# One core, four sequences: context times Wo added to x as a step of its own, z computed from that sum, and the first attention chain in two halves

## Chip, cores, metric

One core of one Trainium2 chip. The metric is the device time of one launch in microseconds. All data is fp32.

## The reference

Four sequences (B = 4) of 512 tokens with 256 features. Cut to what matters:

```python
# 1. conditioned adapter: h = x + relu(x @ w_down[b]) @ w_up[b], both weights scaled and shifted from cond[b]
# 2. attention on h: paths = sigmoid(h @ Wp + bp); similarity from 5 levels, causal softmax, 8 heads
x = x + (softmax(sim) @ (h @ Wv)) @ Wo
# 3. y = x @ (U[b] @ V) + bias, with U[b] = cond[b] @ W_dec + b_dec, K = 30 inner columns
# 4. each token goes to the expert e with the largest score of y
x = x + y + y @ expert_w[e].T
```

The kernel folds 3 and 4 into a narrow vector z = x @ U + ub of 30 (padded to 32) columns: scores come from z, and the outcome for expert e is z @ G[e], with G[e] = V + V @ expert_w[e].T.

## The kernel before, in words

Everything is kept transposed: features on partitions, tokens on the free axis. `x_t` holds x and, at the end, the output. One list, `ORDER`, fixes the order of all steps, and each of the engines runs through that same list and does its part of each step. So the order of the steps in `ORDER` (built by `after_scores`, `after_context` and a few fixed lists, L76 to L147) is the order of work on each engine.

Attention of a batch is cut into six pairs of key tiles (`PAIRS`, L35), so pair p runs from 0 to 23 and batch b begins at pair 6b. For each: `scores` (TensorE into `s_ps`), Exp (ScalarE into `prob`, L365), where needed a causal mask (GpSimd, L342) or the sum `tiles` (VectorE, "add", L509), and `context` (TensorE into `c_ps`). Four of the six contexts of a batch end a chunk; VectorE then normalises it (reciprocal L420, product L421 into `ctx_t`). Between scores(p+1) and context(p), and behind context(p), stand the other steps, listed in the gaps:

- `gdn`, `gup`: the scaled adapter weights `w_dn`, `w_up` (VectorE adds and multiplies, L432 to L450). `down`, `up`: the adapter, `h_t` on VectorE (L455). `up` comes as two steps, one for each half of the rows of 64.
- `VL`: values and logits of 128 tokens, copied by ScalarE (L377). `bias`, `tanh`, `feat`: logits to 32 products for each head and token (VectorE L464, ScalarE L383, VectorE L549 and L552). `phi`: their transposes for four heads, scaled by ScalarE into `phi_t` (L390). `scores` reads `phi_t`.
- `U`, `Uadd`, `ubT`, `Q`, `G`, `WoU`: once, the weights of the second part. `U` needs W_dec and goes through DRAM. `WoU` is Wo times U.
- `zT`: z of the batch from `x_t` with U and from `ctx_t` with `WoU` (L712), so it needs no sum x + ctx Wo. `zs`: z by token and scores, then on VectorE the copy `z_nat` and the choice (`smax`, `hit`, `key`, `kmax`, `pick`, L519 to L526). `zo`: z placed at the chosen expert (GpSimd, in the last batch VectorE). `zoT`: its transposes, copied by ScalarE to `zo_t` (L402).
- `out` 0 to 3: for one of two feature halves and one of two token halves, `ctx_t` times Wo and `zo_t` times G accumulated in one bank; VectorE adds it to `x_t` in place (L541), and SP stores it.

A step that isn't scores or context writes a PSUM bank. Behind the start only two banks are left for them, taken in turn (`WORK`, L149 to L158). TensorE waits before a step until the last user of its bank has been emptied (`emptied`), that is read by VectorE or ScalarE. In the start four banks of `s_ps` serve as well (`EARLY_BANK`); scores(0) waits until they are emptied.

## Time and profile before

| | us |
|---|---|
| median of 3 runs | 154.97 (154.96 to 156.26) |
| the profiled execution | 155.55 |
| its span | 153.4 |

| engine | busy us | share |
|---|---|---|
| TensorE | 141.2 | 92% |
| VectorE | 83.7 | 55% |
| ScalarE | 58.8 | 38% |
| GpSimd | 31.2 | 20% |

The profiled execution is one run; its span is the time from the first to the last event on the core, and 2.15 us lie around it. PE is TensorE, PEld its weight loads, DVE VectorE, ACT ScalarE, POOL GpSimd, SP the engine that issues loads and stores. Matmuls all go through helper functions, so they carry line L561 and are told apart by their tiles: `work<-w_vl,h_t` is VL, `work<-ctx_t,mix_sb` the first half of `out`, `work<-zo_t,gexp` its second half. Each fp32 matmul shows as two rows, except transposes. Their ends are modelled and run on into the next step, so the length of a step is best read from start to start. "idle before <- X" says what ended the engine's wait.

### The profile page before, as it was taken

How to read it: one execution, taken by the hardware profiler on the slowest of the kernel's cores; microseconds unless marked ns; L12 is line 12 of the kernel's file. 1: busy time of each engine (PE TensorE's matmuls, PEld its weight loads, DVE VectorE, ACT ScalarE, POOL GpSimd, SP SyncE). 2: the span in 40 equal slices, each digit the busy share in tenths (PEclk: the TensorE clock that was granted, in tenths of full speed). 3: DMA queues.
4: the chain of work that ended last, by engine and by line, in shares of the span. 5: the costliest groups of instructions: out<-in, count | busy, mean ns of one | idle time of the engine just before them, and what ended most of it. 6: DMA issues, size and time to landing. Idle time of an engine off the chain costs nothing.

```text
span 153.4 us, 5078 instructions
## 1 busy us (share of the span) xinstructions
PE 141.2 (92%) x2296; PEld 89.8 (59%) x2296; DVE 83.7 (55%) x156; ACT 58.8 (38%) x70; POOL 31.2 (20%) x56
## 2 busy tenths in 40 slices
PE   5989678999497999999999999999999999999992
PEld 5746155554274777457656655567558577666650
DVE  0563532619966378296915483558146851985431
ACT  3013156264226342558333451573434447310010
POOL 7200004100405302640022205200222440110000
...
GB/s 121 311 320 433 448 376 353 209 4 0 0 22 17 35 0 4 0 4 0 37 3 38 34 4 0 38 0 4 34 38 38 0 38 0 38 38 34 68 38 71
DMA packets 7381, 12.50 MB, mean 81 GB/s; under 512 B 1552, under 2 KB 5808, under 8 KB 7232
## 3 DMA queue, kind: packets, MB, share of 16 engines
...
q0 software_dynamic: 96, 0.05, 1.1%
...
q14 instruction: 3, 0.02, 0.1%
...
## 4 chain that ended last, share of the span: by engine, by line
PE 83%; DVE 11%; ACT 2%; issue 1%; POOL 0%; ACTq 0%; POOLq 0%; DVEq 0%
PE work L561 36%; PE c_ps L561 24%; PE s_ps L561 17%; PE work L738 3%; DVE rden L420 2%; DVE feat L552 2%; PE work L678 2%; DVE tiles L509 1%; ACT prob L365 1%; DVE h_t L455 1%; ACT phi_t L390 1%; DVE u_row L481 1%; PE work L730 1%; DVE x_t L541 1%; DVE logit L464 0%
## 5 line engine op out<-in xcount | busy, mean ns | idle before, releaser
L365 ACT ACTIVATE prob<-s_ps 128x1536 f32<-128x1536 f32 (+1 forms) x24 | 38.2, 1593 | 39.3 <-PE s_ps L561 36.3
L420 DVE RECIPROCAL rden<-c_ps 128x256 f32<-128x256 f32 x16 | 28.1, 1757 | 26.5 <-PE c_ps L561 26.5
L342 POOL TENSOR_SCALAR_AFFINE_SELECT prob<-prob 128x1024 f32<-128x1024 f32 x16 | 20.1, 1257 | 93.1 <-ACT prob L365 93.1
L561 PE MATMUL s_ps<-phi_t 32*128 32x256 f32 (+1 forms) x384 | 24.2, 365 | 1.6 <-ACT phi_t L390 1.0
L561 PE MATMUL c_ps<-prob,v_sb 128*32 128x256 f32 (+1 forms) x384 | 24.9, 346 | 0.0
L561 PEld LDWEIGHTS s_ps<-phi_t 32*128 32x128 f32 x384 | 17.4, 184 | 10.6 <-issue 6.8
L561 PE MATMUL work<-ctx_t,mix_sb 128*32 128x256 f32 x256 | 17.0, 381 | 0.4
L561 PE MATMUL work<-zo_t,gexp 128*32 128x256 f32 x256 | 16.9, 379 | 0.0
L561 PEld LDWEIGHTS c_ps<-prob,v_sb 128*32 128x32 f32 x384 | 11.5, 109 | 9.0 <-issue 2.0
L561 PE MATMUL c_ps<-prob,ones 128*32 128x256 f32 (+1 forms) x256 | 16.3, 326 | 0.0
L561 PE MATMUL work<-w_vl,h_t 128*32 128x296 f32 x208 | 14.8, 416 | 1.1 <-DVE h_t L455 0.6
L541 DVE TENSOR_TENSOR x_t<-work,x_t 128x256 f32<-128x256 f32 x16 | 6.7, 419 | 13.3 <-PE work L561 13.3
L561 PEld LDWEIGHTS work<-zo_t,gexp 128*32 128x32 f32 x256 | 8.6, 110 | 5.2 <-ACT zo_t L402 0.2
L561 PEld LDWEIGHTS work<-ctx_t,mix_sb 128*32 128x32 f32 x256 | 7.8, 110 | 4.9 <-ACT phi_t L390 1.2
L509 DVE TENSOR_TENSOR tiles<-prob 128x1024 f32<-128x1024 f32 x8 | 10.6, 1329 | 0.0
L561 PEld LDWEIGHTS work<-w_vl,h_t 128*32 128x32 f32 x208 | 6.1, 109 | 7.1 <-DVE pick L526 1.6
L561 PEld LDWEIGHTS c_ps<-prob,ones 128*32 128x32 f32 x256 | 8.0, 110 | 2.7
L350 POOL TENSOR_TENSOR zo<-z_nat,pick 128x256 f32<-128x256 f32 x12 | 7.0, 615 | 9.8 <-DVE pick L526 9.8
L377 ACT COPY v_sb<-work 128x296 f32<-128x296 f32 x13 | 5.2, 403 | 9.6 <-PE work L561 9.6
L455 DVE TENSOR_TENSOR h_t<-work,x_t 128x512 f32<-128x512 f32 x6 | 3.9, 686 | 8.2 <-PE work L561 8.2
L402 ACT COPY zo_t<-work 128x512 f32<-128x512 f32 x8 | 4.4, 590 | 8.4 <-PE work L738 8.4
L421 DVE TENSOR_TENSOR ctx_t<-c_ps,rden 128x256 f32<-128x256 f32 x16 | 6.8, 424 | 0.6
...
## 6 DMA issues: line engine op xcount, KB each, us to landing
...
```

The lines of the kernel that those rows point to most:

```text
L342: nc.gpsimd.affine_select(out=tri, in_=tri, compare_op=ALU.is_ge, fill=0.0, base=0, pattern=[[0, HG], [0, 2], [1, P]], channel_multiplier= ...
L350: ins = nc.gpsimd.tensor_tensor(zo[:, t], z_nat[:, t:t + 1, :].broadcast_to([P, E, KP]), pick[:, t, :].unsqueeze(2).broadcast_to([P, E, KP ...
L365: nc.scalar.activation(prob[:, p % 2, :, 0:width(p)], s_ps[:, :, 0:width(p)], ACT.Exp).then_inc(exped, 1)
L377: nc.scalar.copy(v_sb[:, b % 2, t, :], bank(s)[:, 0:D + H * DEPTH]).then_inc(empty(s), 1)
L402: nc.scalar.copy(zo_t[:, :, CW * s[2]:CW * (s[2] + 1)], bank(s)[:].rearrange("p (e t) -> p e t", e=2)).then_inc(empty(s), 1)
L420: link(nc.vector.reciprocal(rden[:], c_ps[m % 2][:, CW:2 * CW]))
L421: nc.vector.tensor_tensor(ctx_t[:, b % 2, g, CW * half:CW * (half + 1)], c_ps[m % 2][:, 0:CW], rden[:], ALU.mult).then_inc(ctx_ready, 1)
L455: nc.vector.tensor_tensor(h_t[:, :, half], bank(s)[:].rearrange("p (c t) -> p c t", c=DC), x_t[:, b, :, half], ALU.add).then_inc(empty(s), 1)
L509: nc.vector.tensor_tensor(tiles[:, chunk(p) % 2], both[:, :, 0, :], both[:, :, 1, :], ALU.add).then_inc(added, 1)
L541: nc.vector.tensor_tensor(x_t[:, b, c, half], bank(s)[:, 0:CW], x_t[:, b, c, half], ALU.add).then_inc(empty(s), 1)
L561: return nc.tensor.matmul(o, w, r, start=start, stop=stop, skip_group_check=True)
L738: ins = nc.tensor.transpose(o[:, CW * e + P * i:CW * e + P * (i + 1)], zo[:, 2 * hf + i, 4 * e:4 * e + 4, :].rearrange("p e k -> p (e k)") ...
```

## The change

- `WoU`, its transposed copy of Wo and the `ctx_t` half of `zT` are gone. `out` is cut in two steps. `mix` multiplies `ctx_t` by Wo and adds the result to `x_t` in place; `zT` reads `x_t` once all `mix` steps of its tokens have been added; `out` holds only `zo_t` times G, and adds again. Each `mix` and `out` takes a bank and a VectorE add.
- The first batch's `bias`, `tanh`, `feat` and `phi` come in two halves, for the first and the last 256 tokens. The first pair of scores needs only the first. The second half's `phi` stand behind scores 1, in front of `up` of batch 1.
- Scaling of `phi` goes to VectorE for group 1 in all batches, and for both groups of the first batch's second half.
- `gdn` of batches 1 to 3 runs as two VectorE instructions of 384 columns in place of six of 128, and stands before `up`; `gup` 1 stands behind it. `gup` 2 and 3 move out of the start into batch 0. `U`, `G` and VL of batch 1 change their gaps.
- W_dec, mix and the expert weights are loaded on SP's queue behind x of batch 1, and no longer by ScalarE behind its first `down`; x of batches 2 and 3 follow them. mix is 256 KB smaller.
- Eight warm-up products in place of nine, and the two banks are taken in the other turn.

```diff
-WARM = 9
+WARM = 8
...
-PROLOGUE = [("gdn", (0,)), ("gup", 0), ("down", 0), ("gup", 1), ("up", 0, 0), ("up", 0, 1), ("gdn", (1, 2, 3)),
-            ("VL", 0, 0), ("VL", 0, 1), ("VL", 0, 2), ("VL", 0, 3), ("bias", 0), ("tanh", 0), ("feat", 0),
-            ("gup", 2), ("gup", 3), ("phi", 0, 0), ("phi", 0, 1), ("scores", 0), ("down", 1)]
-EARLY_BANK = {("gdn", (0,)): 0, ("gup", 0): 1, ("down", 0): 2, ("gup", 1): 3, ("up", 0, 0): 4, ("up", 0, 1): 5,
-              ("gdn", (1, 2, 3)): 0, ("VL", 0, 0): 1, ("VL", 0, 1): 2, ("VL", 0, 2): 3, ("VL", 0, 3): 4,
-              ("gup", 2): 0, ("gup", 3): 1, ("phi", 0, 0): 5, ("phi", 0, 1): 2}
+def part(b, ts):
+
+    return 1 if ts == FIRST else b + 2
+
+
+def scaler(s):
+
+    return "scalar" if s[2] == 0 and s[3] != SECOND else "vector"
+
+
+def features(b, ts):
+
+    return [("bias", b, ts), ("tanh", b, ts), ("feat", b, ts)]
+
+
+PROLOGUE = [("gdn", (0,)), ("gup", 0), ("down", 0), ("gdn", (1, 2, 3)), ("up", 0, 0), ("up", 0, 1), ("gup", 1),
+            ("VL", 0, 0), ("VL", 0, 1), *features(0, FIRST), ("VL", 0, 2), ("VL", 0, 3), ("bias", 0, SECOND),
+            ("phi", 0, 0, FIRST), ("phi", 0, 1, FIRST), ("tanh", 0, SECOND), ("scores", 0), ("feat", 0, SECOND),
+            ("down", 1)]
+EARLY_BANK = {("gdn", (0,)): 0, ("gup", 0): 1, ("down", 0): 2, ("gdn", (1, 2, 3)): 3, ("up", 0, 0): 4, ("up", 0, 1): 5,
+              ("gup", 1): 0, ("VL", 0, 0): 1, ("VL", 0, 1): 2, ("VL", 0, 2): 4, ("VL", 0, 3): 5,
+              ("phi", 0, 0, FIRST): 1, ("phi", 0, 1, FIRST): 2}
 def after_scores(b):
...
-        gaps[4] += [("phi", n1, 0), ("phi", n1, 1)]
+        gaps[4] += [("phi", n1, 0, ALL_T), ("phi", n1, 1, ALL_T)]
     if b == 0:
-        gaps[1] += [("VL", n1, 2), ("VL", n1, 3)]
-        gaps[2] += [("U", 1)]
+        gaps[0] = [("phi", b, 0, SECOND), ("phi", b, 1, SECOND)] + gaps[0]
+        gaps[1] += [("U", 1)]
+        gaps[2] += [("VL", n1, 2), ("VL", n1, 3)]
         gaps[3] += [("U", 3)]
-        gaps[5] += [("G", 1), ("Uadd",)]
+        gaps[5] += [("gup", 3), ("Uadd",)]
     elif n1 < B:
         gaps[1] += [("zs", prv, ALL_T), ("zo", prv, 0), ("zo", prv, 1), ("VL", n1, 0), ("VL", n1, 1)]
         gaps[2] += [("VL", n1, 2), ("VL", n1, 3)]
@@ -101,6 +118,7 @@
         gaps[1] += [("zs", prv, ALL_T), ("zo", prv, 0), ("zo", prv, 1)]
         gaps[4] += [("zs", b, FIRST), ("zo", b, 0)]
     if prv >= 0:
+        gaps[0] += [("mix", prv, 2), ("mix", prv, 3)]
...
 def after_context(b):
...
-        gaps[0] += [("VL", n1, 0), ("VL", n1, 1)]
-        gaps[1] += [("bias", n1), ("tanh", n1), ("U", 0), ("feat", n1)]
-        gaps[2] += [("U", 2)]
-        gaps[3] += [("Q",)]
-        gaps[4] += [("G", 0), ("ubT",)]
-        gaps[5] += [("down", n2), ("WoU",)]
+        gaps[0] += [("U", 0)]
+        gaps[1] += [("VL", n1, 0), ("VL", n1, 1)]
+        gaps[2] += features(n1, ALL_T) + [("U", 2)]
+        gaps[3] += [("Q",), ("gup", n2)]
+        gaps[4] += [("G", 0), ("ubT",), ("mix", b, 0)]
+        gaps[5] += [("G", 1), ("down", n2), ("mix", b, 1)]
     else:
         gaps[0] += [("zT", prv, ALL_T)]
-        gaps[3] += [("out", prv, 0)]
-        gaps[4] += [("out", prv, 1)]
-        gaps[5] += [("out", prv, 2)]
+        gaps[2] += [("mix", b, 0), ("mix", b, 1)]
     if b >= 1 and n1 < B:
-        gaps[2] += [("bias", n1), ("tanh", n1), ("feat", n1)]
-    if prv >= 1:
-        gaps[1] += [("out", prv - 1, 3)]
+        gaps[2] += features(n1, ALL_T)
+        gaps[3] += [("out", prv, 0), ("out", prv, 1)]
+        gaps[4] += [("out", prv, 2)]
+        gaps[5] += [("out", prv, 3)]
     if b >= 1 and n2 < B:
         gaps[5] += [("down", n2)]
     if b == B - 1:
-        gaps[2] += [("zT", b, FIRST)]
-        gaps[5] = [("zoT", b, 0), ("out", prv, 2), ("out", prv, 3)]
+        gaps[3] += [("zT", b, FIRST), ("out", prv, 0)]
+        gaps[4] += [("out", prv, 1)]
+        gaps[5] += [("zoT", b, 0), ("out", prv, 2), ("out", prv, 3)]
...
-ORDER += [("zT", B - 1, SECOND), ("out", B - 1, 0), ("zs", B - 1, SECOND), ("zo", B - 1, 1),
-          ("out", B - 1, 1), ("zoT", B - 1, 1), ("out", B - 1, 2), ("out", B - 1, 3)]
+ORDER += [("out", B - 1, 0), ("mix", B - 1, 2), ("mix", B - 1, 3), ("out", B - 1, 1), ("zT", B - 1, SECOND),
+          ("zs", B - 1, SECOND), ("zo", B - 1, 1), ("zoT", B - 1, 1), ("out", B - 1, 2), ("out", B - 1, 3)]
...
-        _k, _late = _late % 2, _late + 1
+        _k, _late = 1 - _late % 2, _late + 1
...
-            for b in range(1, B):
+            sp.dma_start(x_t[:, 1], x_tr[1].rearrange("(c p) t -> p c t", p=P)).then_inc(ld_x[1], 16)
+            sp.dma_start(wdec[:], W_dec).then_inc(ld_wdec, 16)
+            sp.dma_start(mix_sb[:], mix).then_inc(ld_mix, 16)
+            sp.dma_start(ex_t[:], expert_tr.rearrange("e (c p) f -> p e c f", p=P)).then_inc(ld_ex, 16)
+            for b in range(2, B):
                 sp.dma_start(x_t[:, b], x_tr[b].rearrange("(c p) t -> p c t", p=P)).then_inc(ld_x[b], 16)
...
-                    if s[1] == 0:
-                        act.dma_start(wdec[:], W_dec).then_inc(ld_wdec, 16)
-                        act.dma_start(mix_sb[:], mix).then_inc(ld_mix, 16)
-                        act.dma_start(ex_t[:], expert_tr.rearrange("e (c p) f -> p e c f", p=P)).then_inc(ld_ex, 16)
...
-                elif s[0] == "phi":
-                    _, b, g = s
-                    if b == 0 and g == 0:
+                elif s[0] == "phi" and scaler(s) == "scalar":
+                    _, b, g, ts = s
+                    tok = slice(P * ts[0], P * (ts[-1] + 1))
+                    if b == 0:
                         act.wait_ge(rootc_ready, 1)
                     full(act, s)
-                    nc.scalar.activation(phi_t[:, b % 2, g, :], bank(s)[:], ACT.Copy, scale=rootc[:]
+                    nc.scalar.activation(phi_t[:, b % 2, g, tok], bank(s)[:, tok], ACT.Copy, scale=rootc[:]
...
-                    for b in s[1]:
-                        ins = nc.vector.tensor_tensor(w_dn[:, b], dproj[:],
-                                                      g[:, b:b + 1, 0:HD].broadcast_to([P, DC, HD]), ALU.mult)
-                    link(ins)
-                    for b in s[1]:
-                        ins = nc.vector.tensor_tensor(w_dn[:, b], w_dn[:, b],
-                                                      g[:, b:b + 1, HD:2 * HD].broadcast_to([P, DC, HD]), ALU.add)
-                    ins.then_inc(empty(s), 1)
+                    bs, n = slice(s[1][0], s[1][-1] + 1), len(s[1])
+                    link(nc.vector.tensor_tensor(w_dn[:, bs], dproj[:].unsqueeze(1).broadcast_to([P, n, DC, HD]),
+                                                 g[:, bs, 0:HD].unsqueeze(2).broadcast_to([P, n, DC, HD]), ALU.mult))
+                    nc.vector.tensor_tensor(w_dn[:, bs], w_dn[:, bs],
+                                            g[:, bs, HD:2 * HD].unsqueeze(2).broadcast_to([P, n, DC, HD]), ALU.add
+                                            ).then_inc(empty(s), 1)
...
+                elif kind == "phi" and scaler(s) == "vector":
+                    _, b, g, ts = s
+                    tok = slice(P * ts[0], P * (ts[-1] + 1))
+                    full(dve, s)
+                    nc.vector.tensor_scalar(phi_t[:, b % 2, g, tok], bank(s)[:, tok], rootc[:], None, op0=ALU.mult
+                                            ).then_inc(empty(s), 1)
...
-                elif kind == "WoU":
-                    full(dve, s)
...
-                elif kind == "out":
+                elif kind in ("mix", "out"):
...
-                        done(pe, ("WoU",))
-                    pe.wait_ge(ctx_ready, BC * b + (NG if ts == FIRST else BC))
-                    for c in range(2 * DC):
+                        pe.wait_ge(u_ready, 1)
+                    for i in range(TT):
+                        if i // DC in (t // 2 for t in ts):
+                            done(pe, ("mix", b, i))
+                    for c in range(DC):
                         for t in ts:
-                            tok = slice(P * t, P * (t + 1))
-                            w = u_w[:, c, b, :] if c < DC else wo_u[:, c - DC, KP * b:KP * (b + 1)]
-                            r = x_t[:, b, c, tok] if c < DC else ctx_t[:, b % 2, c - DC, tok]
-                            ins = mm(o[KP * t:KP * (t + 1), 0:P], w, r, start=(c == 0), stop=(c == 2 * DC - 1))
+                            ins = mm(o[KP * t:KP * (t + 1), 0:P], u_w[:, c, b, :], x_t[:, b, c, P * t:P * (t + 1)],
+                                     start=(c == 0), stop=(c == DC - 1))
...
-                elif kind == "out":
+                elif kind in ("mix", "out"):
                     _, b, i = s
-                    if b == 0 and i == 0:
-                        done(pe, ("G", 0))
-                        done(pe, ("G", 1))
                     row, half = slice(P * (i % DC), P * (i % DC + 1)), slice(CW * (i // DC), CW * (i // DC + 1))
-                    for c in range(2 * DC):
-                        if c == DC:
-                            done(pe, ("zoT", b, i // DC))
-                        w = wo[:, c, row] if c < DC else gexp[:, c - DC, row]
-                        r = ctx_t[:, b % 2, c, half] if c < DC else zo_t[:, c - DC, half]
-                        ins = tiled(o[:, 0:CW], w, r, start=(c == 0), stop=(c == 2 * DC - 1))
+                    if kind == "mix":
+                        if b == 0 and i == 0:
+                            pe.wait_ge(ld_mix, 16)
+                        pe.wait_ge(ctx_ready, BC * b + NG * (i // DC + 1))
+                    else:
+                        if b == 0 and i == 0:
+                            done(pe, ("G", 0))
+                            done(pe, ("G", 1))
+                        done(pe, ("zoT", b, i // DC))
+                    for c in range(DC):
+                        w = wo[:, c, row] if kind == "mix" else gexp[:, c, row]
+                        r = ctx_t[:, b % 2, c, half] if kind == "mix" else zo_t[:, c, half]
+                        ins = tiled(o[:, 0:CW], w, r, start=(c == 0), stop=(c == DC - 1))
```

## Rows read from the trace of the kernel before

**Rows 1.** The page: busy us, share of the span, instructions, of TensorE.

```profile
PE 141.2 (92%) x2296; PEld 89.8 (59%) x2296; DVE 83.7 (55%) x156; ACT 58.8 (38%) x70; POOL 31.2 (20%) x56
```

**Rows 2.** Waits, whole span: row waited for; us in total, times, longest.

```profile
PE work L561 <- DVE u_row L481: 2.2, 1, 2.2
...
PE work L678 <- DVE q_bd L470: 1.0, 1, 1.0
...
PE work L561 <- DVE pick L526: 0.5, 2, 0.2
```

**Rows 3.** Timeline of the start: start, duration, engine, tiles, count, idle before and releaser.

```profile
11.66 1.21 PE L561 MATMUL work<-w_vl,h_t 128*32 128x296 f32 x16 [0.59 <-DVE h_t L455]
...
15.78 1.98 PE L561 MATMUL work<-lift_sb,cond_b 128*128 128x512 f32 x4
...
15.91 0.41 ACT L377 COPY v_sb<-s_ps 128x296 f32<-128x296 f32 x1 [0.59 <-PE s_ps L561]
...
19.26 1.06 PE L678 MATMUL s_ps<-ident,feat 128*128 128x128 f32 x8 [1.50 <-DVE feat L552]
...
21.31 0.94 PE L561 MATMUL s_ps<-phi_t 32*128 32x256 f32 x16 [0.98 <-ACT phi_t L390]
...
25.75 0.64 PE L561 MATMUL c_ps<-prob,v_sb 128*32 128x256 f32 x8
```

**Rows 4.** Groups by shape, VectorE: busy us, mean ns; idle before.

```profile
L541 DVE TENSOR_TENSOR x_t<-work,x_t 128x256 f32<-128x256 f32 x16 | 6.7, 419 | 13.3 <-PE work L561 13.3
```

**Rows 5.** Timeline from the end of batch 0 into batch 1.

```profile
54.20 1.06 PE L561 MATMUL work<-u_w,mix_sb 128*32 128x128 f32 x32
...
55.18 0.94 PE L561 MATMUL s_ps<-phi_t 32*128 32x256 f32 x16
...
56.05 1.26 PE L561 MATMUL work<-act_t,w_up 64*128 64x256 f32 x8
...
57.21 1.29 DVE L455 TENSOR_TENSOR h_t<-work,x_t 128x512 f32<-128x512 f32 x2 [1.08 <-PE work L561]
...
57.24 0.64 PE L561 MATMUL c_ps<-prob,v_sb 128*32 128x256 f32 x8
...
58.82 1.76 DVE L420 RECIPROCAL rden<-c_ps 128x256 f32<-128x256 f32 x1 [0.32 <-PE c_ps L561]
...
59.00 0.62 PE L561 MATMUL work<-ctx_t,wo_u 128*32 128x128 f32 x16
...
62.48 1.20 PE L561 MATMUL work<-w_vl,h_t 128*32 128x296 f32 x16 [0.24 <-DVE pick L526]
```

**Rows 6.** The page: GB/s of all transfers in 40 slices of 3.8 us.

```profile
GB/s 121 311 320 433 448 376 353 209 4 0 0 22 17 35 0 4 0 4 0 37 3 38 34 4 0 38 0 4 34 38 38 0 38 0 38 38 34 68 38 71
```

**Rows 7.** Timeline: the two halves of one `out` step.

```profile
72.62 1.05 PE L561 MATMUL work<-ctx_t,mix_sb 128*32 128x256 f32 x16
...
73.49 1.05 PE L561 MATMUL work<-zo_t,gexp 128*32 128x256 f32 x16
```

**Rows 8.** Timeline of the last batch, where GpSimd and VectorE meet.

```profile
133.79 1.10 POOL L342 TENSOR_SCALAR_AFFINE_SELECT prob<-prob 128x1024 f32<-128x1024 f32 x1 [7.31 <-ACT prob L365]
...
133.81 1.10 DVE L524 TENSOR_TENSOR key<-hit,rank 128x16 f32<-128x16 f32 x1
```

**Rows 9.** Timeline of the tail.

```profile
136.98 0.66 PE L738 MATMUL work<-ident,zo 128*128 128x128 f32 x4
...
144.25 0.23 DVE L519 COPY z_nat<-work 128x64 f32<-128x64 f32 x1
...
145.42 0.76 DVE L534 TENSOR_TENSOR zo<-z_nat,pick 128x256 f32<-128x256 f32 x2
...
146.99 0.59 ACT L402 COPY zo_t<-work 128x512 f32<-128x512 f32 x1 [4.48 <-PE work L738]
...
150.61 0.42 DVE L541 TENSOR_TENSOR x_t<-work,x_t 128x256 f32<-128x256 f32 x1 [1.30 <-PE work L561]
```

**Rows 10.** Stretch: length, busy us (count) by engine, granted clock, DMA share, GB/s.

```profile
150.60:153.40 2.80, 0.00 (x0) 0.00 (x0) 0.42 (x1) 0.00 (x0) 0.00 (x0) 0.90 0.15 50
```

67 lines of the change are left out of this document (31 added, 36 removed).

## Prediction, made before the changed kernel was seen

> **What bounds the kernel now.** I read the page first: TensorE is busy for 92% of the span [rows 1], and no other engine comes near. So two things count: how much TensorE has to do, and where it stands still. The list of its waits names the places: 2.2 us for VectorE's copies of `u_row` and 1.0 for `q_bd`, both in batch 0, and 0.5 in two waits of 0.24 for `pick`, one each at the start of batches 2 and 3's VL steps [rows 2]. The timeline of the start shows one more: before the first scores at 21.31 TensorE waits for one long chain, and two `gup` products at 15.78 fill part of that wait for nothing [rows 3]. Behind batch 0 the matmuls follow each other closely, so the rest of the span is almost pure TensorE time.
>
> **Start: the chain is halved.** Four VL steps run from 11.66 to the last copy at 15.91, so one is about 1.0 us, with 0.25 for the pipeline; copy, bias, tanh and the `feat` operations then take until the transposes at 19.26, 3.35 us [rows 3]. Now two VL steps are enough: the copy starts at 11.66 + 2.25 = 13.9. The chain behind it works on half the columns; a little under half of it grows with columns, so I take 2.65 us. In front of it I count 0.3 sooner: one warm-up product less, and `gup` 1 (1.0, half of the 1.98 at 15.78) no longer ahead of `up`, against `w_dn` of three batches that now is, on VectorE. Transposes start at 16.25. From there to the scores took 21.31 - 19.26 = 2.05; half the columns, and a scaling on each of two engines, make it 1.25. First scores: **17.5, 3.8 sooner**. VectorE's scaling of 256 columns isn't in the trace: it lies between 0.42, the in-place add of 256 columns [rows 4], and 0.65, half of the 1.29 of two `h_t` of 512 columns [rows 5]; it is nearest to the first, and I take 0.42.
>
> From the first scores to the first context product took 25.75 - 21.31 = 4.4. The exponential between them stays as it is; the transposes of the second half (0.5), their scaling (0.4, which `up` waits for, as it needs the bank) and the stagger of the second `up` behind the second scaling (0.45) come in: 5.8. First context product at 23.35, **gain 2.4**. Loads: W_dec now stands in SP's queue behind `x` of batch 1. Up to its end 5.8 MB have to move, which at the rates of the slices shown takes until about 19 us [rows 6]; it is wanted first at 24.9. Cost nothing, with 5 us to spare; each us later than 24.9 would count in full.
>
> **TensorE's work.** `WoU` goes: 55.18 - 54.20, with a little before it, 0.9. `zT` loses its `ctx_t` half, 0.62 less the 0.19 by which a row runs on into the next step (1.05 against 73.49 - 72.62): 0.43 in each of five steps, 2.1 [rows 5, 7]. Together 3.0 less. `out` is cut into `mix` and `out`, 0.87 each [rows 7]: no more work, but 16 more adds of 0.42 on VectorE, 6.7 us [rows 4]. `gup` 2 and 3 leave the idle stretch of the start for the full stream: 1.9 more. So TensorE gains only 1 us behind the start. What decides is the waits: every step needs one of two banks, and a bank comes free when VectorE, strictly in order, has emptied it.
>
> **Batch 0, first context product to scores 7** (before 55.18 - 25.75 = 29.4). Work: two `gup` +1.8, `mix` 0 and 1 +1.7, `WoU` -0.9: +2.6. Waits that go: `u_row` 2.2 with 0.3 beside it, `q_bd` 1.0 [rows 2], 0.3 of small ones: -3.8. New ones: a normalisation (reciprocal 1.76, product 0.42) begins 1.6 after its context product does, 58.82 - 57.24 [rows 5]. `phi` 0 of batch 1 needs the bank of `Q`, emptied behind the normalisation and the `q_bd` copies: 0.75; `phi` 1 that of `gup` 2: 0.4. `mix` 0 needs the bank of `G` 0, an add of 0.42 and its latency: 0.6. `mix` 1 needs the bank of `G` 1, whose add stands behind the normalisation of context 5: 0.2 + 2.2 + 0.45 after that context ends, while TensorE has 1.75 to do: 1.1. Sum 2.85. In all 1.65; VectorE operations with two SBUF inputs that meet a mask may add up to 0.9 each [rows 8]. I take **+2.0**.
>
> **Batch boundary, twice** (scores 7 and 13). `up` starts at 56.05, `h_t` at 57.21, 0.65 for each half; before, context follows at 57.24 without any of it [rows 5]. Now `mix` 2 needs the first `h_t` to have emptied its bank, at 57.9 against 57.15: 0.8 with the wake-up. `zT` behind it is 0.43 shorter, but the second VL step waits for `pick`, the end of a VectorE chain from the normalisation at 58.82; the matmul at 62.48 already waited for it [rows 2, 5], so in both batches the 0.43 only lengthens that wait. Scores 7 to 13: two `mix` behind `up` and two of the next batch, less one full `out` that moves on, +1.7; wait 0.8: **+2.5**. Scores 13 to 19: as much work as before, 0.8, 0.3 because `up` needs the bank of `out` 3, whose add stands behind a normalisation, and 0.1 at `phi`: **+1.2**.
>
> **Last batch** (scores 19 to the end of context 23). Work -0.9 (`zT` of batch 2, first `zT` of batch 3). Waits where `out` used to cover and a half step doesn't: `mix` 2 of batch 2 behind the normalisation of context 17, 0.65; scores 21 behind an exponential, 0.3; `mix` 0 behind the normalisation of context 19, 0.6; context 23 behind its mask, 0.55: **+1.2**.
>
> **Tail** (before 150.61 + 0.42 - 136.98 = 14.05 [rows 9]). `zoT`, six half steps and a wait of 0.5 for a bank: 6.3. Then `zT` 0.45, and nothing is left to cover: `z_t` 0.7, `zs` 0.45, `z_nat` to the end of `zo` 145.42 + 0.76 - 144.25 = 1.93, `zoT` 0.7, `zo_t` 0.6 with 0.05, two halves to the last add 0.87 + 1.1 + 0.45: 13.6. **-0.4**, although TensorE has 3.5 us less to do there.
>
> **Sum.** -2.4 + 2.0 + 2.5 + 1.2 + 1.2 - 0.4 = +4.1. The profiled execution took 155.55 for its span of 153.4, so it would take 159.65; the median of the three runs, 154.97, is 0.6 lower. I forecast **159.0**.
>
> **Two rules weighed.** In the last batch `key`, an operation on 16 columns with two SBUF inputs, took 1.10 us beside GpSimd's mask of 1.10 [rows 8]. The Trainium skill (SBUF — State Buffer, "SBUF: two separate sides") has VectorE and GpSimd take a shared port pair as a lock, and the trace agrees. By that rule the 16 new adds, with one input in PSUM, are not held, and the sum is as it stands; without it up to 0.9 more for each that meets a mask.
>
> From 150.60 to 153.40 the granted clock is 0.90 on average, so TensorE fell from 2.4 to 1.2 GHz in it, after its last matmul [rows 10]; the waits for `u_row` did not do it. In the new tail it does 1.1 us of work in 4.6 before the last two steps; a fall there costs 2 x 0.87 = 1.7. The Trainium skill (TensorE: Matmul & The Clock Gate, Part 1) has an idle TensorE sent back to half rate, which speaks against such a tail.
>
> **Rivals.**
> *The clock falls in the tail*: 160.7. For it the idle tail; against it, that 2.2 us at a stretch did not suffice. Chance 0.13.
> *The new waits at `mix` do not appear*, as VectorE empties the banks early; it decides from about 0.8 us sooner than worked out. 0.6 + 1.1 + 0.8 + 0.8 + 0.65 + 0.6 = 4.5 less: 154.5, not slower. For it: VectorE has idle time before most normalisations. Against: `h_t` at 57.21 and the normalisation in front of the adds. Chance 0.18.
> *TensorE's stream alone counts*: the 1.15 at `phi` and 2 us of the tail's chain vanish too: 151.4. Against it: the tail has nothing to put there. Chance 0.12.
> *The start gives nothing*, as a load is late: 2.4 more, 161.4. Chance 0.05.
> *As forecast*: 0.52, with a range of its own of 157.3 to 160.5.
>
> A measurement of this kernel can tell about 1% from no change. Faster than 153.4: the third and 0.02 of the second, 0.14. Within 1%: the rest of the second and 0.02 of the last, 0.18. Slower: 0.68. The range leaves out most of the third case and the fourth: 153.8 to 160.8.
>
> **What would show it.** First scores near 17.5, first context product near 23.4. No wait for `u_row`; waits of 0.8 for `h_t` before `mix` 2 and of 1.1 for `gexp` before `mix` 1; those for `pick` grown from 0.24 to 0.7. In the tail one idle stretch of 2 us between `zs` and `zoT`. What would make me wrong: each wait is a small difference of two sums of several us, so a step that runs 0.5 us otherwise on VectorE moves it by as much, in batch 0 and in the last batch above all.

## The result and the profile after

| | before | changed |
|---|---|---|
| median, us (lowest to highest, runs) | 155.09 (154.96 to 156.26, 4) | 160.26 (159.41 to 160.60, 4) |
| span of the profiled execution, its own time | 153.4, 155.55 | 158.2, 160.25 |
| mean granted clock of TensorE in it | 0.998 | 0.989 |

The changed kernel takes 1.031 times as long, with a 95% interval of 1.024 to 1.037: slower. The forecast was 159.0, with a range of 153.8 to 160.8.

The page of the kernel after, first part, the row that answers to [rows 1] (busy us, share of the span, instructions):

```profile
PE 140.9 (89%) x2198; PEld 86.7 (55%) x2198; DVE 92.4 (58%) x179; ACT 56.4 (36%) x67; POOL 31.6 (20%) x56
```

TensorE is busy for as long as before (141.2), in a span 4.8 longer, and 1.45 of the 140.9 is slow running in the tail (below). So the time went into standing still, and into those 1.45. The waits of the kernel after, over the whole span (us in total, times, longest), against [rows 2]:

```profile
PE work L754 <- DVE zo L553: 2.1, 1, 2.1
PE work L582 <- DVE h_t L471: 1.9, 3, 0.8
...
PE work L582 <- DVE gexp L517: 1.3, 2, 0.9
PE work L582 <- DVE ctx_t L439: 1.0, 2, 0.7
PE work L582 <- DVE pick L545: 1.0, 2, 0.5
PE work L582 <- ACT zo_t L420: 0.8, 1, 0.8
```

The 2.2 us for `u_row` are gone. In these rows seven small waits have come, two each for `h_t`, `gexp` and `ctx_t` on VectorE and one for ScalarE's `zo_t`, and one of 2.1 in the tail; the two for `pick` have grown.

The timeline of the start, after, against [rows 3] (start, duration, engine, tiles, count, idle before and releaser):

```profile
11.04 1.21 PE L582 MATMUL work<-w_vl,h_t 128*32 128x296 f32 x16 [0.40 <-DVE h_t L471]
...
16.00 0.41 PE L701 MATMUL work<-ident,feat 128*128 128x128 f32 x2 [0.76 <-DVE feat L572]
...
17.20 0.94 PE L582 MATMUL s_ps<-phi_t 32*128 32x256 f32 x16 [0.58 <-DVE phi_t L488]
...
23.04 0.64 PE L582 MATMUL c_ps<-prob,v_sb 128*32 128x256 f32 x8
```

The first scores are 4.1 sooner, the first context product 2.7. The same view from the end of batch 0 into batch 1, against [rows 5]:

```profile
46.05 1.07 PE L582 MATMUL work<-ctx_t,mix_sb 128*32 128x256 f32 x16 [0.40 <-DVE gexp L517]
...
53.58 1.07 PE L582 MATMUL work<-ctx_t,mix_sb 128*32 128x256 f32 x16 [0.94 <-DVE gexp L517]
54.58 0.94 PE L582 MATMUL s_ps<-phi_t 32*128 32x256 f32 x16
...
57.36 1.93 PE L582 MATMUL work<-ctx_t,mix_sb 128*32 128x256 f32 x32 [0.77 <-DVE h_t L471]
```

Scores 7 begins at 54.58, 0.6 ahead of before's 55.18: 2.1 of the 2.7 are given back within batch 0. The last batch:

```profile
119.11 1.94 PE L582 MATMUL work<-ctx_t,mix_sb 128*32 128x256 f32 x32 [0.70 <-DVE ctx_t L439]
...
125.86 0.94 PE L582 MATMUL s_ps<-phi_t 32*128 32x256 f32 x16 [0.16 <-ACT prob L385]
...
128.13 1.93 PE L582 MATMUL work<-ctx_t,mix_sb 128*32 128x256 f32 x32 [0.34 <-DVE ctx_t L439]
...
138.97 0.64 PE L582 MATMUL c_ps<-tiles,ones 128*32 128x256 f32 x8 [0.54 <-issue]
```

And the tail, against [rows 9], with the granted clock of its stretches (length, busy us and count by engine, clock, DMA share, GB/s), against [rows 10]:

```profile
140.84 0.66 PE L754 MATMUL work<-ident,zo 128*128 128x128 f32 x4
...
150.77 0.63 PE L754 MATMUL work<-ident,zo 128*128 128x128 f32 x4 [2.12 <-DVE zo L553]
...
152.16 3.38 PE L582 MATMUL work<-zo_t,gexp 128*32 128x256 f32 x32 [0.77 <-ACT zo_t L420]
...
155.60 0.42 DVE L560 TENSOR_TENSOR x_t<-work,x_t 128x256 f32<-128x256 f32 x1 [1.02 <-PE work L582]
```

```profile
150.60:151.70 1.10, 0.63 (x4) 0.42 (x4) 0.02 (x1) 0.27 (x1) 0.00 (x0) 1.00 0.00 0
151.70:155.20 3.50, 3.04 (x32) 1.61 (x32) 0.42 (x1) 0.32 (x1) 0.00 (x0) 0.51 0.00 0
155.20:158.20 3.00, 0.34 (x8) 0.00 (x0) 0.42 (x1) 0.00 (x0) 0.00 (x0) 1.00 0.25 87
```

The two last half steps took 3.38 instead of about 1.9, at a granted clock of 0.51: the rival of the clock in the tail has come true. In [rows 10] the clock fell too, but when no product was left.

All profiles are read below by the same seven stages. They are start times of TensorE's rows in the timeline and, for the end, the end of the last `x_t` add:

| us | first scores at | to first context | to scores 7 | to scores 13 | to scores 19 | to the last batch's first `zoT` | to the last add |
|---|---|---|---|---|---|---|---|
| before | 21.31 | 4.44 | 29.43 | 29.56 | 30.29 | 21.95 | 14.05 |
| changed | 17.20 | 5.84 | 31.54 | 31.81 | 31.08 | 23.37 | 15.18 |
| e1_start_only | 16.81 | 5.83 | 29.98 | 29.43 | 30.29 | 21.95 | 14.06 |
| e2_split_only | 21.03 | 4.44 | 31.00 | 31.79 | 31.09 | 23.36 | 15.89 |
| e3_swap_g | 17.50 | 5.83 | 30.39 | 31.81 | 31.08 | 23.36 | 15.90 |
| e4_tail_filled | 17.11 | 5.83 | 31.54 | 31.80 | 31.08 | 23.37 | 15.52 |
| e5_tail_filled_less | 18.16 | 5.83 | 31.54 | 31.80 | 31.09 | 23.37 | 13.77 |
| e6_banks_and_clock | 17.25 | 5.83 | 30.40 | 31.94 | 31.22 | 23.36 | 13.77 |
| e7_start_and_order | 16.81 | 5.83 | 28.79 | 29.44 | 30.30 | 21.94 | 14.06 |
| e8_tail_out_late | 18.21 | 5.84 | 31.53 | 31.80 | 31.09 | 23.36 | 13.70 |
| e9_mix_late | 17.86 | 5.83 | 30.39 | 31.18 | 30.51 | 24.12 | 13.78 |
| e10_start_order_2 | 17.58 | 5.83 | 28.51 | 29.95 | 30.81 | 21.95 | 14.06 |
| e11_loads_scalar | 17.11 | 5.84 | 31.54 | 31.80 | 31.09 | 23.37 | 15.30 |
| e12_start_order_3 | 18.02 | 5.84 | 28.51 | 29.44 | 30.29 | 21.95 | 14.05 |

Three things are to be seen in it. Kernels that have the same order in a stage agree in it within 0.02, as long as the clock holds. The first column, for one and the same start, moves between 16.8 and 18.2 from one execution to the next. So differences below 1 us between medians mean little here, and stages of the profiles are compared instead. And the play of the start lies ahead of one row: from the end of the first `gup` product (at 6.64 in the changed kernel, its row is in the last section) to the first scores, every profile of the new start takes 10.55 to 10.70, and the two of the old start, before and e2, take 14.24.

### The profile page after: what moved, and what is told of

It reads as the page before. It is cut to its first block, busy times and chain, and to the rows that moved or that the text cites. A ratio compares the mean times of both kernels' runs of the same rounds, so it can differ in the third digit from the quotient of the medians.

```text
span 158.2 us, 4939 instructions
## 1 busy us (share of the span) xinstructions
PE 140.9 (89%) x2198; PEld 86.7 (55%) x2198; DVE 92.4 (58%) x179; ACT 56.4 (36%) x67; POOL 31.6 (20%) x56
## 4 chain that ended last, share of the span: by engine, by line
PE 67%; DVE 24%; issue 3%; DMA 3%; ACT 2%; DVEq 0%
PE work L582 31%; PE c_ps L582 19%; PE s_ps L582 12%; DVE rden L438 11%; DMA first_sb<-in_first 3%; PE work L754 2%; PE work L701 2%; DVE ctx_t L439 2%; DVE h_t L471 2%; DVE x_t L560 1%; ACT prob L385 1%; DVE feat L572 1%; DVE u_w L512 1%; DVE phi_t L488 1%; DVE w_up L464 1%
## 5 line engine op out<-in xcount | busy, mean ns | idle before, releaser
L362 POOL TENSOR_SCALAR_AFFINE_SELECT prob<-prob 128x1024 f32<-128x1024 f32 x16 | 20.9, 1303 | 89.6 <-ACT prob L385 89.6
L560 DVE TENSOR_TENSOR x_t<-work,x_t 128x256 f32<-128x256 f32 x32 | 13.3, 422 | 18.8 <-PE work L582 18.8
L582 PE MATMUL work<-ctx_t,mix_sb 128*32 128x256 f32 x256 | 15.6, 381 | 3.9 <-DVE h_t L471 1.5
L582 PE MATMUL work<-zo_t,gexp 128*32 128x256 f32 x256 | 17.7, 408 | 1.0 <-ACT zo_t L420 0.8
L582 PEld LDWEIGHTS c_ps<-prob,v_sb 128*32 128x32 f32 x384 | 12.0, 110 | 8.5 <-issue 1.4
L528 DVE TENSOR_TENSOR tiles<-prob 128x1024 f32<-128x1024 f32 x8 | 9.9, 1240 | 0.0
L416 ACT ACTIVATE z_t<-work,ub_col 128x128 f32<-128x128 f32 (+1 forms) x5 | 1.8, 365 | 17.3 <-PE work L582 17.3
L572 DVE TENSOR_TENSOR feat<-feat,sign 128x64 f32<-128x64 f32 (+4 forms) x20 | 7.2, 359 | 0.7
## 6 DMA issues: line engine op xcount, KB each, us to landing
wdec<-in_W_dec SPq DMA_DIRECT2D x1, 3855.0 KB, 17.9
```

Of the source, the lines that this page charges most:

```text
L362: nc.gpsimd.affine_select(out=tri, in_=tri, compare_op=ALU.is_ge, fill=0.0, base=0, pattern=[[0, HG], [0, 2], [1, P]], channel_multiplier= ...
L528: nc.vector.tensor_tensor(tiles[:, chunk(p) % 2], both[:, :, 0, :], both[:, :, 1, :], ALU.add).then_inc(added, 1)
L560: nc.vector.tensor_tensor(x_t[:, b, c, half], bank(s)[:, 0:CW], x_t[:, b, c, half], ALU.add).then_inc(empty(s), 1)
L572: ins = nc.vector.tensor_tensor(feat[:, rows, n:2 * n], feat[:, rows, 0:n], sign[:, rows, i:i + 1].broadcast_to([P, H * len(ts), n]), ALU. ...
L582: return nc.tensor.matmul(o, w, r, start=start, stop=stop, skip_group_check=True)
```

## The experiments

### The two halves apart: e1_start_only and e2_split_only

The first has the start, the loads and the order of batch 0 of the change, with the attention output as before; the second the reverse. In the first:

```diff
-        gaps[5] += [("G", 1), ("down", n2), ("mix", b, 1)]
+        gaps[5] += [("G", 1), ("down", n2), ("WoU",)]
...
-        gaps[0] += [("mix", prv, 2), ("mix", prv, 3)]
```

> The kernel before with the first half of the change alone: halved first chain, loads issued by SyncE, the changed kernel's order of batch 0 (with gup 2 and 3 in it); context times Wo, WoU, zT and out as in the kernel before. My theory (the two halves of the change add up, and this one is a gain): first context product near 23.0, 2.7 sooner than before; in batch 0 gup 2 and 3 cost 2.1, the waits at phi 0.8, and the old waits for u_row and q_bd (2.2 + 1.0) are gone, so scores 7 still 2.7 sooner, near 52.5, and nothing behind it changes: 152.4 us. Rival (the start only moves waiting time into batch 0, where TensorE's stream is full): scores 7 near 54.5, 154.4 us. No wait for gexp in batch 0 and none for h_t before an attention output.

> The kernel before with the second half of the change alone: mix and out as steps of their own, zT from the sum, WoU gone; start, loads and gup as in the kernel before. My theory: first context product at 25.75 as before; batch 0 +1.2 (mix 1.75, WoU -1.0, a wait of 0.4 at mix 0, none at mix 1, since G 1's add is ahead of the normalisation here); scores 7 to 13 +2.2, to 19 +0.8, to the end of context 23 +1.4, tail -0.5 and +1.7 if the clock falls as it did in the changed kernel: 160.3 us at full clock, 162.0 with the fall. Rival (the split costs only its waits of 0.8, 0.7 and 0.3, since TensorE has less to do): 157 us.

Measured: 152.87 us and 162.78 us, against 155.85 for the kernel before on the same chip. The ratios are 0.984 (0.980 to 0.989) and 1.047 (1.043 to 1.050). By stages the halves add up: to scores 7 +0.55 and +1.57 make 2.12 against the 2.11 of the change; to scores 13 and 19 the second half alone gives +2.23 and +0.80, against +2.25 and +0.79. The whole loss is the second half's, and waits for a bank are only part of it. From the first context product to the last batch's `zoT` e2 is 6.0 longer. Counted from start to start, four half steps of 0.87 (3.5) move in from the tail, and `WoU` (1.0) and four `ctx_t` halves of `zT` (0.43 each) go: 0.8 more work. The other 5.2 are waits. What the four steps leave behind is TensorE's busy time in the tail (the second number), here before and in e8 (below), where the clock held:

```profile
136.98:151.03 14.05, 13.38 (x223) 8.39 (x219) 6.43 (x16) 1.53 (x3) 0.00 (x0) 1.00 0.17 58
```

```profile
141.83:155.53 13.70, 9.94 (x151) 5.53 (x147) 7.07 (x18) 1.53 (x3) 0.00 (x0) 1.00 0.14 49
```

TensorE has 3.4 less to do there, and the tail is only 0.35 shorter, because the chain over `z_t`, `zo` and `zo_t` on the other engines sets it now. In e2 itself the clock fell, and its tail is 1.84 longer.

The first half is a gain of 2.5 by the ratio: 4.5 sooner at the first scores, of which it gives back 1.4 by the first context product and 0.55 in batch 0 (0 expected), and nothing later. It changes the start in several ways at once (halves, `gup` moved, scaling on VectorE, loads), and no run here takes them apart, but for the loads (e11). The rival "it only moves waiting time" falls with scores 7 at 52.6, and so does the 157 of "the split costs only its waits". The second half alone cost 0.8 more than expected: 0.4 in batch 0 and 0.6 in a tail in which the clock fell earlier, less 0.3 by an earlier start. One wait that I had expected away stayed in the first kernel, in front of WoU, and so was no price of `mix`:

```profile
51.61 1.08 PE L587 MATMUL work<-u_w,mix_sb 128*32 128x128 f32 x32 [0.94 <-DVE gexp L522]
```

### A wait for a bank: e3_swap_g

```diff
-        gaps[5] += [("G", 1), ("down", n2), ("mix", b, 1)]
+        gaps[5] += [("down", n2), ("G", 1), ("mix", b, 1)]
```

> The changed kernel with G 1 and down 2 exchanged behind context 5, so that mix 1 takes the bank that ScalarE empties and not that of G 1, whose add stands behind a normalisation on VectorE. My theory (a wait for a bank is lost time on TensorE): the wait of 0.94 for gexp is gone and everything behind is 0.9 sooner, 159.3 us. Rival (VectorE's queue is the bound there, and the wait moves to the up or mix 2 behind it): scores 7 is 0.9 sooner but context 6 is not, 160.3 us.

Measured: 160.31 us, ratio to before 1.028 (1.023 to 1.033), which by itself looks like the rival. The stages say otherwise: to scores 7 took 30.39 instead of 31.54, 1.15 less, and the three stages between it and the tail did not give it back. Two things hid it: first scores that came 0.3 later, and a tail of 15.90 instead of 15.18, because here the clock fell ahead of `zoT` and not behind it. The windows of its tail:

```profile
148.00:150.00 2.00, 0.10 (x1) 0.14 (x2) 1.58 (x8) 0.00 (x0) 0.00 (x0) 0.85 0.06 20
150.00:152.00 2.00, 1.23 (x8) 0.81 (x12) 0.00 (x0) 0.59 (x1) 0.00 (x0) 0.50 0.00 0
152.00:154.00 2.00, 2.00 (x24) 1.04 (x20) 0.26 (x1) 0.00 (x0) 0.00 (x0) 0.50 0.00 0
```

The wait's row had said 0.94, and its removal gave 1.15. The row counts from the modelled end of the product before (1.05 long), while in a stream the next one starts 0.87 after its start. So this wait cost its row and about 0.2 more.

### The clock in the tail: e4_tail_filled, e5_tail_filled_less, e8_tail_out_late

Products into a bank that is no longer read, behind three steps:

```diff
+FILL = {("zT", B - 1, SECOND): 4, ("zs", B - 1, SECOND): 14, ("zoT", B - 1, 1): 5}
...
+                for _ in range(FILL.get(s, 0)):
+                    mm(c_ps[0][:, 0:P], ident[:], ident[:])
```

> The changed kernel with 4, 14 and 5 products of 128 columns into a bank that is no longer read, behind the last zT, zs and zoT: they fill TensorE's three idle stretches of the tail (0.55, 2.12 and 0.77). Theory of the clock (the last two half steps took 3.38 for 1.73 because the granted clock had fallen): the clock stays at 1.00, the last two half steps take 1.73, 158.6 us. Rival (the two steps are slow for another reason, such as the DMAs or the adds beside them): they still take 3.4 and the time is 160.3 us, or more where the added products stand in the way.

Measured: 161.10 us, not faster, ratio 1.034 (1.031 to 1.038). But the clock held at 1.00 and the last two half steps took 1.93. What failed was my size of a product. Rows of its tail:

```profile
148.96 3.39 PE L584 MATMUL c_ps<-ident 128*128 128x128 f32 x28
...
153.83 1.93 PE L584 MATMUL work<-zo_t,gexp 128*32 128x256 f32 x32
```

Fourteen products took 3.39 and not 1.8, since each is 0.24 (two records each). `zoT` began 1.5 later in the tail than in the changed kernel (152.18 - 140.73 against 150.77 - 140.84). With half as many:

```diff
-FILL = {("zT", B - 1, SECOND): 4, ("zs", B - 1, SECOND): 14, ("zoT", B - 1, 1): 5}
+FILL = {("zT", B - 1, SECOND): 2, ("zs", B - 1, SECOND): 7, ("zoT", B - 1, 1): 3}
```

> The changed kernel with 2, 7 and 3 products of 128 columns behind the last zT, zs and zoT instead of 4, 14 and 5. In the run before, 14 of them took 3.39 us and not 1.8, and held up the zoT behind them by about 1.1; by that row one takes 0.24, so 7 end 0.2 to 0.3 ahead of zo. Theory of the clock: granted clock 1.00 to the last product, the last two half steps in 1.93 instead of 3.38, nothing held up: 158.6 us. Rival (the fall costs less than it seems, since the end hangs on something else than these two steps): 160.3 us.

Measured: 158.46 us, ratio 1.021 (1.017 to 1.026), where 158.6 was expected. The tail is 13.77, and this is its end:

```profile
153.15 1.93 PE L584 MATMUL work<-zo_t,gexp 128*32 128x256 f32 x32
...
155.14 0.42 DVE L562 TENSOR_TENSOR x_t<-work,x_t 128x256 f32<-128x256 f32 x1 [0.44 <-PE work L584]
```

From `zoT` to the last add 13.77 instead of 15.18: the fall of the clock costs 1.41, and nothing but the added products differs. In all six executions the mean clock was 1.00. The profiled one is a slow one of them, at 159.85, because its first scores came at 18.16.

Real work in the same place:

```diff
-ORDER += [("out", B - 1, 0), ("mix", B - 1, 2), ("mix", B - 1, 3), ("out", B - 1, 1), ("zT", B - 1, SECOND),
-          ("zs", B - 1, SECOND), ("zo", B - 1, 1), ("zoT", B - 1, 1), ("out", B - 1, 2), ("out", B - 1, 3)]
+ORDER += [("out", B - 1, 0), ("mix", B - 1, 2), ("mix", B - 1, 3), ("zT", B - 1, SECOND),
+          ("zs", B - 1, SECOND), ("zo", B - 1, 1), ("out", B - 1, 1), ("zoT", B - 1, 1), ("out", B - 1, 2), ("out", B - 1, 3)]
```

> The changed kernel with the out step 1 of the last batch put behind the last zs instead of in front of the last zT: real work in the longest idle stretch of the tail, which shrinks from 2.12 to about 1.3. By the sum of the tail zs starts 0.2 sooner. If this much work keeps the clock up, the last two half steps take 1.93: 158.4 us. If it does not, 160.1 us; by what the trace of the changed kernel shows, where three stretches of 0.55, 2.12 and 0.77 lay in 4.6 us, I can't tell, and take the fall as likelier.

Measured: 160.09 us, ratio 1.028 (1.024 to 1.032). The profiled execution kept its clock, and its tail took 13.70:

```profile
151.71 0.63 PE L754 MATMUL work<-ident,zo 128*128 128x128 f32 x4 [1.11 <-DVE zo L553]
...
153.11 1.94 PE L582 MATMUL work<-zo_t,gexp 128*32 128x256 f32 x32 [0.77 <-ACT zo_t L420]
```

In four of the six executions the mean clock was 0.989 all the same, as in three of the four of the changed kernel. So one half step of 0.87 in the idle stretch of 2.1 does not secure the clock, and whether it helps at all can't be told: it held in two of six executions here and in one of four without it. The order by itself gained next to nothing, 13.70 against the 13.77 of the filled tail.

### Can the waits be ordered away? e6_banks_and_clock and e9_mix_late

Both have the filled tail and the exchange of G 1 and down 2. The first also puts `mix` 2 in front of `up`:

```diff
-        gaps[0] += [("mix", prv, 2), ("mix", prv, 3)]
+        gaps[0] = [("mix", prv, 2)] + gaps[0] + [("mix", prv, 3)]
```

> The changed kernel with the tail filled by 2, 7 and 3 products, G 1 and down 2 exchanged behind context 5, and mix 2 of the batch before put in front of up instead of behind it, so that it no longer takes the bank from which h_t is added. My theory (each wait for a bank is lost in full on TensorE): against the kernel with the filled tail, 1.15 sooner at scores 7 by the exchange, and 0.4 at each of the two batch boundaries, as the wait of 0.77 for h_t leaves about 0.35 at mix 3 and up 1: 156.6 us. Rival (VectorE's chain behind the boundary sets the time, and the wait for pick grows by what the boundary gains): 157.4 us.

Measured: 158.59 us, ratio 1.018 (1.015 to 1.022), in an interval that overlaps that of the filled tail alone. The exchange gave its 1.14 again. The boundary gave nothing: to scores 13 took 31.94 instead of 31.80. To scores 19 took 31.22 instead of 31.09. Its timeline shows where the 0.77 went:

```profile
54.34 1.07 PE L584 MATMUL work<-ctx_t,mix_sb 128*32 128x256 f32 x16
55.34 1.74 PE L584 MATMUL work<-act_t,w_up 64*128 64x256 f32 x8
57.25 1.07 PE L584 MATMUL work<-ctx_t,mix_sb 128*32 128x256 f32 x16 [0.17 <-DVE h_t L473]
```

The wait in front of `mix` 3 is 0.17, but the eight rows of `up` now stretch over 1.74 instead of 1.14. By the turn of the banks the second `up` needs the one of `mix` 2, whose add ended at 55.90. The merged row doesn't name this wait; that it is this one is read from the order. Both my theory (0.4 less for each boundary) and the rival (`pick` grows; it stayed at 0.48) were wrong. With two banks the wait went to the step between.

The second puts both `mix` behind the context product, `zT` behind the next scores, and `zs` between the two VL steps:

```diff
-        gaps[0] += [("zT", prv, ALL_T)]
+        gaps[0] += [("mix", prv, 2), ("mix", prv, 3)]
...
-        gaps[1] += [("zs", prv, ALL_T), ("zo", prv, 0), ("zo", prv, 1), ("VL", n1, 0), ("VL", n1, 1)]
+        gaps[1] += [("zT", prv, ALL_T), ("VL", n1, 0), ("zs", prv, ALL_T), ("zo", prv, 0), ("zo", prv, 1),
+                    ("VL", n1, 1)]
...
-        gaps[1] += [("zs", prv, ALL_T), ("zo", prv, 0), ("zo", prv, 1)]
+        gaps[1] += [("zT", prv, ALL_T)]
...
+    if b == B - 1:
+        gaps[1] += [("zs", prv, ALL_T), ("zo", prv, 0), ("zo", prv, 1)]
```

The last batch has no VL steps; there `zs` and `zo` of batch 2 now stand one context product later.

> The changed kernel with all its waits behind batch 0 aimed at: tail filled by 2, 7 and 3 products, G 1 and down 2 exchanged, mix 2 and 3 of the batch before behind the first context and no longer behind up, zT behind the next scores, and zs between the first two VL steps, so that the second of these no longer takes zs's bank. My theory (the split costs mostly its waits, and they can be ordered away): scores 7 to 13 falls from 31.81 to about 30.6 (0.77 and 0.48 go), scores 13 to 19 by no more than 0.2, scores 19 on 0.7 sooner; with 1.15 from the exchange 158.5 - 1.15 - 2.5 - 0.7 = 154.2 us. Rival (as when mix 2 was put ahead of up, the waits move to the next user of the bank): scores 7 to 13 stays near 31.5, 157 us.

Measured: 157.69 us, ratio 1.012 (1.008 to 1.016): nearer to the rival's 157 than to my 154.2. To scores 13 and 19 took 31.18 and 30.51, 0.62 and 0.58 less, where I had expected 1.2 and 0.2. The two waits of 0.77 and 0.48 are gone, two others came, and one in the last batch:

```profile
60.62 0.65 PE L586 MATMUL work<-x_t,u_w 128*32 128x128 f32 x16 [0.29 <-DVE x_t L564]
...
62.63 0.30 PE L750 MATMUL work<-ident,z_t 128*128 128x128 f32 x1 [0.37 <-ACT z_t L420]
...
130.12 0.63 PE L758 MATMUL work<-ident,zo 128*128 128x128 f32 x4 [0.52 <-POOL zo L374]
```

`zT` waits for the add of `mix` 3, which stands behind a normalisation on VectorE; `zs` waits for ScalarE, which is in an exponential; and in the last batch GpSimd's `zo`, moved behind a context product, is late. The stage to `zoT` became 0.75 longer, where 0.7 less was expected from scores 19 on. So aiming at the waits took 0.6 off at each boundary and left the kernel 1.2% above the one before. What better orders would give is open.

### The gaining half, improved: e7_start_and_order, e10_start_order_2, e12_start_order_3

All have the first half alone and the exchange. The first adds an early Q:

```diff
-        gaps[5] += [("G", 1), ("down", n2), ("WoU",)]
+        gaps[5] += [("down", n2), ("G", 1), ("WoU",)]
...
-        gaps[3] += [("Q",), ("gup", n2)]
+        gaps[3] += [("gup", n2)]
...
-        gaps[2] += [("VL", n1, 2), ("VL", n1, 3)]
+        gaps[2] += [("VL", n1, 2), ("VL", n1, 3), ("Q",)]
```

> The kernel with the first half of the change alone, and two moves in batch 0: G 1 and down 2 exchanged, so that WoU takes the bank that ScalarE empties (a wait of 0.94 for gexp goes), and Q put ahead of context 2, so that phi 0 doesn't wait for its copies (0.58). My theory: scores 7 is 1.15 + 0.4 sooner and nothing behind it changes: 151.3 us, against 152.9 without the two moves. Rival (the moved copies of Q hold up the features or a normalisation, and another wait takes the place): 152.4 us.

Measured: 152.03 us, ratio 0.978 (0.974 to 0.982). To scores 7 took 28.79 instead of 29.98, 1.19 less: the exchange's 1.15 and nothing for Q, because `gup` 2's add, behind the same normalisation, was next:

```profile
42.55 0.66 PE L706 MATMUL work<-ident,feat 128*128 128x128 f32 x4 [0.63 <-DVE w_up L466]
```

Then `gup` 2 went along with Q, into 2.15 us in which VectorE had been idle, and `zs` between the VL steps:

```diff
-        gaps[2] += [("VL", n1, 2), ("VL", n1, 3), ("Q",)]
+        gaps[2] += [("VL", n1, 2), ("VL", n1, 3), ("Q",), ("gup", 2)]
...
-        gaps[3] += [("gup", n2)]
+        gaps[3] += []
...
-        gaps[1] += [("zs", prv, ALL_T), ("zo", prv, 0), ("zo", prv, 1), ("VL", n1, 0), ("VL", n1, 1)]
+        gaps[1] += [("VL", n1, 0), ("zs", prv, ALL_T), ("zo", prv, 0), ("zo", prv, 1), ("VL", n1, 1)]
```

> The first half of the change alone, with G 1 and down 2 exchanged, Q and gup 2 both ahead of context 2, where VectorE is idle for 2.15, and zs between the first two VL steps. In the run before, the wait of 0.58 for Q's copies had only become one of 0.63 for gup 2's. My theory: that one goes too, and the two waits of 0.24 for pick: scores 0 to 7 in 34.0 instead of 34.6, scores 7 to 13 in 29.2 instead of 29.4; 151.0 us. Rival (VectorE has 0.8 more in front of the features and the copies of u_row, and the next wait takes the place): 152.0 us, as before the two moves.

Measured: 152.91 us, ratio 0.982 (0.979 to 0.985). Batch 0 gained 0.28: scores 0 to 7 took 34.34, where 34.0 was expected, though no wait is left there behind the first context product. Each boundary lost 0.51, since VL's second step now waits for ScalarE's copy of the first, which stands behind an exponential:

```profile
59.61 1.20 PE L587 MATMUL work<-w_vl,h_t 128*32 128x296 f32 x16 [0.75 <-ACT v_sb L394]
```

So I took the second move back and kept the first:

```diff
-        gaps[1] += [("VL", n1, 0), ("zs", prv, ALL_T), ("zo", prv, 0), ("zo", prv, 1), ("VL", n1, 1)]
+        gaps[1] += [("zs", prv, ALL_T), ("zo", prv, 0), ("zo", prv, 1), ("VL", n1, 0), ("VL", n1, 1)]
```

> The first half of the change alone, with G 1 and down 2 exchanged and Q and gup 2 ahead of context 2, but with zs in front of both VL steps, as in the kernel before. In the run before, batch 0 had no wait left behind its first context product, but the moved zs made the second VL step wait 0.75 for a copy of ScalarE instead of 0.24 for pick. My theory (the two moves don't touch each other): scores 0 to 7 in 34.3 as there, scores 7 to 13 in 29.4 as in the kernel before, so from the first scores to the end of the span 132.2, 0.3 less than with Q alone moved; 151.7 us with the start as it usually falls. Rival (the changed turn of the two banks brings a wait of its own at the boundary): scores 7 to 13 over 29.6.

Measured: 152.01 us (151.14 to 152.40), ratio 0.976 (0.973 to 0.979). Its stages are 28.51 and 29.44, both as expected. From the first scores to the end of the span it takes 132.2, against 132.5 with Q alone moved. From the first scores on it is the fastest of the kernels with the new start, by 0.3, which the medians (152.01 and 152.03) can't show. It beats both given ones: 2.4% under the one before, where the changed one is 3.1% above it.

### Who issues the loads: e11_loads_scalar

```diff
-            sp.dma_start(wdec[:], W_dec).then_inc(ld_wdec, 16)
...
+                    if s[1] == 0:
+                        act.dma_start(wdec[:], W_dec).then_inc(ld_wdec, 16)
```

(and so for `mix_sb` and `ex_t`).

> The changed kernel with W_dec, mix and the expert weights loaded by ScalarE behind its first down step, as in the kernel before, and not by SyncE. My theory (moving the loads cost and gained nothing, since W_dec is there 5 us before it is wanted): first scores 17.2 to 18.2 and first context product 5.84 behind them, no wait at U 0, 160.3 us. Rival (part of the gain at the start came from the loads: ScalarE no longer issues three of them in front of its VL copies): first scores 0.3 or more later.

Measured: 160.22 us, ratio 1.028 (1.026 to 1.031). First scores at 17.11, context products 5.84 behind, every stage up to the tail within 0.01 of the changed kernel. From the end of the first `gup` product to the first scores it took 10.55, against 10.56, so the play of the start hides nothing: moving the loads cost and gained nothing. The reason given was too wide, though. W_dec, issued at 2.71, landed 17.9 us later and so about 3 us before the changed kernel's first `U` (24.36), not 5; issued by ScalarE at 7.6, with 14.9 to landing, it had about 2.

## Why the prediction was nearly right, step by step

The sum of the forecast against the stages of the profiled executions:

| | forecast | measured |
|---|---|---|
| first context product | -2.4 | -2.71 |
| to scores 7 | +2.0 | +2.11 |
| to scores 13 | +2.5 | +2.25 |
| to scores 19 | +1.2 | +0.79 |
| to the last batch's `zoT` | +1.2 | +1.42 |
| tail | -0.4 | +1.13 |
| sum | +4.1 | +4.99 |

**Start.** The transposes began at 16.00 (forecast 16.25) and took 1.20 to the scores (1.25); from there to the context product took 5.84 (5.8). VectorE's scaling of 256 columns, bounded by 0.42 and 0.65, took 0.48. Where first scores falls depends on the execution (last section). Counted from the end of the first `gup` product, which takes that play out, the first context product comes 10.56 + 5.84 behind it, against 14.24 + 4.44 before: 2.28 sooner. The other 0.43 of the 2.71 lie ahead of it, one warm-up product less and the chance of the execution; the forecast of -2.4, with its share for the warm-up product, fits. The loads cost nothing: no wait stood in front of U 0, and e11 confirms it, with about 3 us to spare and not 5.

**Batch 0.** The waits are best compared by how much later than in a stream a step began. `mix` 0 began 0.61 late (46.05, behind the start of `ubT` at 45.43): forecast 0.6. `mix` 1 began 1.12 late (53.58 - 51.59 - 0.87): forecast 1.1, and its removal gave 1.15. `gup` 2 and 3 cost 1.03 and 1.05, more than the 1.8 put down for both. The allowance for VectorE's adds meeting a mask, 0.35 on top of a computed 1.65, covered that by luck: it stood for another cause. The waits in front of `phi` 0 and 1, put at 0.75 and 0.4, have rows of 0.58 and 0.25. And e1 puts one entry right: the wait in front of the step behind G 1 comes with the new order of batch 0, whatever the step is. I had booked it on `mix`, yet the half with the start alone has it too, and the half with the split alone hasn't.

**Batch boundaries.** By the same count `mix` 2 was 0.84 late in both (57.36 - 55.45 - 1.07, where 1.07 is the step of `up`), forecast 0.8. The wait for `pick` grew by 0.24 to 0.48 and not by the whole 0.43 by which `zT` is shorter: 0.19 too much in each. In the second, `up` was 0.15 late and not 0.3 (87.40 - 86.39 - 0.86), and nothing at `phi`: 0.84 + 0.15 + 0.24 - 0.43 = 0.80, against a measured 0.79. The 0.4 too much there is the sum of small allowances in one direction: 0.19, 0.15 and 0.1 at `phi`.

**Last batch.** By the same count `mix` 2 of batch 2 was 0.78 late (forecast 0.65), scores 21 0.34 (0.3), `mix` 0 0.53 (0.6), context 23 0.71 (0.55). Together 2.36, less 0.87 for two `ctx_t` halves of `zT`: 1.5 against the measured 1.42.

**Tail: the entry that failed.** The sum without a fall of the clock was 13.6; e5 took 13.77 for it, so -0.3 for -0.4. But the clock fell, for 1.41 (e5 against the changed kernel), and I had given that 0.13. The entry in words: "against it, that 2.2 us at a stretch did not suffice". One idle stretch of 2.20 in a busy neighbourhood did not bring the clock down [rows 2, 10]. I carried this over to a tail in which stretches of 0.55, 2.12 and 0.77 leave TensorE 1.05 us of work in 4.5, though I had named just this difference a paragraph before. The rule weighed there (the Trainium skill, TensorE: Matmul & The Clock Gate, Part 1: an idle TensorE goes back to half rate) pointed the right way: the granted clock was 0.51 from 151.70 to 155.20, though TensorE had not been idle throughout. With the stretches filled (e4, e5, e6 and e9) it was 1.00 in all 23 executions. The price of 1.7 was near, a little high because the clock was back at 1.00 some 0.4 before the last product's end.

**The luck in the sum.** The profiled span grew by 4.99 where +4.1 was forecast, and two errors of opposite sign are in that: the stages ahead of the tail came to +3.86 instead of +4.5, and the tail to +1.13 instead of -0.4. Without the fall the profiled execution would have taken 160.25 - 1.41 = 158.8 (the median of e5 is 158.46), close to the forecast of 159.0; with it the median is 160.26, 0.4 from the rival's 160.7. So the time lies in the range given for "as forecast" although a rival of chance 0.13 had come true.

**The rivals.** "The new waits at `mix` do not appear" is refuted by their rows. So is "TensorE's stream alone counts": e3 won 1.15 by a change that left TensorE's work as it was. "The start gives nothing" is refuted by e1.

**The rule of the shared port.** The 32 adds with one input in PSUM took a mean of 422 ns (419 before [rows 4]) and none more than 426. One stood beside GpSimd's mask whole (120.24 to 120.66, the mask from 119.99 to 121.09), so it was not held. The `key` of 16 columns that stood beside the mask took 0.66, and ended within 0.03 of it (137.77 + 1.10 against 138.24 + 0.66), where the other took 0.17. The Trainium skill's rule (SBUF — State Buffer, "SBUF: two separate sides") agrees with both.
